# One four-tile buffer for all eight residual tiles, and a third weight load moved to ScalarE's queue

## What is computed

```python
grouped = x.reshape(b, s // g, g, d)                       # groups of g = 32 tokens
logits = jnp.einsum('bntd,des->bntes', grouped, Wc) + bc + tie
perm = (logits == jnp.max(logits, axis=-3, keepdims=True)) # each expert picks one token per group
permuted = jnp.einsum('bntd,bntes->bnesd', grouped, perm)  # gather
inner = jax.nn.relu(jnp.einsum('bnesd,esdf->bnesf', permuted, W1) + b1)
result_permuted = jnp.einsum('bnesf,esdf->bnesd', inner, W2) + b2
result = jnp.einsum('bnesd,bntes->bntd', result_permuted, perm)  # scatter
x = x + jnp.tanh(g_ffn[0]) * result                        # the residual sum
```

## Time and profile before

| | |
|---|---|
| median of 3 executions | 1777.69 us (1773.9 to 1778.45) |
| time of the profiled execution | 1778.45 us |
| its span in the profile | 1776.7 us |
| TensorE busy | 1663.9 us, 94% |
| VectorE busy | 1335.7 us, 75% |
| expert stage | from about 764 us of the span to its end |
| one iteration of it | about 62 us |

### The profile page before, as it was taken

One profiled execution on the slowest core, in us unless ns is written; L12 is line 12 of the kernel. 1 busy time (PEld: TensorE's weight loads), 2 busy tenths in 40 slices (PEclk: granted clock), 3 DMA queues, 4 the chain that ended last, 5 costly groups with the idle time before them and its releaser, 6 DMA issues.

```text
span 1776.7 us, 53886 instructions
## 1 busy us (share of the span) xinstructions
PE 1663.9 (94%) x23384; PEld 1184.5 (67%) x23384; DVE 1335.7 (75%) x1974; ACT 822.0 (46%) x1073; POOL 623.2 (35%) x847
## 2 busy tenths in 40 slices
PE   7899999999999999979999999999999999999985
PEld 4677777777777777776576567657656765765662
DVE  6777777777777777737788778778877877787776
ACT  3433333333333333445555555565555556555542
POOL 3577777777777777410110011011011101100101
PEclk9999999999999999989999999999999999999997
DMA  7345454545555545353675575576457556645754
GB/s 263 130 144 167 144 173 151 178 151 183 159 167 155 168 144 176 120 187 104 227 238 156 197 247 178 184 236 234 155 200 249 177 194 227 241 150 201 247 180 155
DMA packets 161450, 325.90 MB, mean 183 GB/s; under 512 B 17344, under 2 KB 23232, under 8 KB 155840
## 3 DMA queue, kind: packets, MB, share of 16 engines
q1 hardware_dynamic: 156608, 288.91, 49.9%
q10 hardware_dynamic: 4608, 33.56, 4.8%
HBM read 254.25 MB, written 68.16 MB: 181 GB/s over the span
## 4 chain that ended last, share of the span: by engine, by line
PE 57%; DVE 15%; POOL 10%; issue 9%; ACT 5%; DMA 2%; SPq 0%; DVEq 0%; POOLq 0%; ACTq 0%
PE ps L1309 13%; PE ps L1282 8%; PE ps L1336 8%; PE ps L214 6%; PE ps L844 6%; PE ps L1351 4%; POOL qc L486 4%; POOL qc L487 4%; PE ps L200 4%; PE ps L1331 3%; DVE mx L612 2%; DVE qs L629 2%; PE ps L807 2%; DVE qc L628 2%; PE ps L787 2%
## 5 line engine op out<-in xcount | busy, mean ns | idle before, releaser
L182 POOL TENSOR_TENSOR b_va<-b_mv,eps_layer 128x2 f32<-128x2 f32 x64 | 12.5, 196 | 833.6 <-DVE b_mv L173 832.7
L1194 DVE STREAM_TRANSPOSE res<-res 128x2048 f32<-128x2048 f32 x128 | 292.0, 2295 | 0.1
L1146 ACT ACTIVATE gat<-ps 128x1536 f32<-128x1536 f32 (+1 forms) x128 | 172.2, 1345 | 198.2 <-PE ps L1282 198.2
L787 PE MATMUL ps<-xTh,qh 128*128 128x512 f32 x512 | 208.6, 407 | 7.0 <-DVE qs L629 5.4
L787 PE MATMUL ps<-xTl,qh 128*128 128x512 f32 x512 | 200.2, 391 | 0.0
L787 PE MATMUL ps<-xTh,ql 128*128 128x512 f32 x512 | 199.8, 390 | 0.0
L1216 DVE COPY res<-ps 128x1024 f32<-128x1024 f32 x128 | 156.7, 1224 | 43.7 <-PE ps L1336 43.7
L1282 PE MATMUL ps<-sel,xin 32*128 32x128 f32 x4096 | 153.7, 283 | 27.9 <-ACT sel L242 13.5
L1156 ACT ACTIVATE res<-ps 128x1024 f32<-128x1024 f32 x128 | 131.2, 1025 | 92.8 <-PE ps L1336 92.8
L1282 PEld LDWEIGHTS ps<-sel,xin 32*128 32x128 f32 x4096 | 129.4, 186 | 63.0 <-ACT gat L1146 40.1
L475 POOL TENSOR_TENSOR xTl<-xT,xTh 128x512 fp32r<-128x512 f32 x128 | 160.7, 1286 | 10.9 <-ACT xTh L522 10.9
(11 more groups left out here) (132 smaller groups left out, 3217.1 us busy)
## 6 DMA issues: line engine op xcount, KB each, us to landing
xin<-x_scratch SPq DMA_DIRECT2D x196, 256.0 KB, 4.0
xT<-in_xT SPq DMA_DIRECT2D x32, 1024.0 KB, 5.9
xin<-in_x SPq DMA_DIRECT2D x64, 512.0 KB, 3.8
x_scratch<-xin SPq DMA_DIRECT2D x64, 512.0 KB, 3.1
xin<-in_W SPq DMA_DIRECT2D x128, 256.0 KB, 3.5
gat<-in_W ACTq DMA_DIRECT2D x32, 1024.0 KB, 8.5
xT<-in_W SPq DMA_DIRECT2D x68, 256.0 KB, 4.0
gat<-in_W SPq DMA_DIRECT2D x64, 256.0 KB, 3.8
```

Source lines behind the costliest of these rows:

```text
L787: last = e.matmul(ps[:, 2 + n % 2, :], a[:, c, n * DH:(n + 1) * DH], b[:, c, :], start=(k == 0), stop=(k == len(parts) - 1))
L1146: e.activation(o, v, ACT.Copy).then_inc(m_gaA.sem, 1)
L1194: e.transpose(v, v).then_inc(m_tr.sem, 1)
```

## The change

`NY`, the number of residual tiles with a place in `y`, was already four; now `y`'s four places serve all eight tiles of a batch. Tile t and tile t+4 use the same place, `y[:, t % NY]`. Tile t+4 can only be loaded once tile t has been stored from there. The count of uses, `use(b, t)`, takes the place of the batch number in the semaphores.

`spare(i + 1)` is thus free once the first product of batch i is done, and W2's part 7 is loaded whole by a third DMA on ScalarE's queue, after `t == 5` of the routing loop. `load_third` goes.

On SP the order in an iteration becomes: stores of tiles 0 to 3, loads of tiles 4 to 7, stores of tiles 4 to 7.

Batch 14 (`B - 2`) is an exception: its tiles 4 to 7 go to `xn[:, 0:4]`, and the tiles 4 to 7 of batch 15 go to `xn[:, 4:8]`. All eight are loaded by `load_late` in iteration 15, ahead of the stores, as soon as the last gathers have read `xn`.

```diff
-        NV, NY = route.NV, TH
+        NV, NY = route.NV, 4
...
+        use = lambda b, t: 2 * b + t // NY if b < B - 1 else 2 * B - 3
-        tile_of = lambda b, t: y[:, t] if t < NY else spare(b)[:, (t - NY) * D:(t - NY + 1) * D] if b < B - 1 else xn[:, t]
+        tile_of = lambda b, t: xn[:, t - NY] if b == B - 2 and t >= NY else y[:, t % NY]
...
         def load_second(e, i, u):
-            e.wait_ge(m_w1.sem, m_w1.at(i, 5))
+            e.wait_ge(m_w1.sem, m_w1.at(i, 7 if u == W2_MOVED[2] else 5))
             e.dma_start(second(i, u), w2_dram[u].rearrange("p (k d) -> p k d", d=D)).then_inc(d_room[u].sem, 16)
...
             def load_middle(i, c):
                 if i:
-                    e.wait_ge(d_ys[c].sem, d_ys[c].at(i - 2))
+                    e.wait_ge(d_ys[c].sem, d_ys[c].at(use(i - 2, NY + c)))
                     e.wait_ge(m_w2.sem, m_w2.at(i - 1, 5))
...
             def load_y(b, t):
+                k = use(b, t)
                 if t < NY and live(b + 1):
                     e.wait_ge(m_w1.sem, m_w1.at(b + 1, piece(b + 1, W1_MIDDLE)))
-                    if b:
-                        e.wait_ge(d_ys[t].sem, d_ys[t].at(b - 1))
-                elif t < NY:
-                    e.wait_ge(d_ys[t].sem, d_ys[t].at(b - 1))
-                elif live(b + 1):
-                    e.wait_ge(m_w1.sem, m_w1.at(b + 1, 7))
-                else:
-                    e.wait_ge(m_gap.sem, m_gap.at(b, 2 * C - 1))
-                e.dma_start(tile_of(b, t), batch(x1_dram, b, t, 1)[:, 0]).then_inc(d_yl[t].sem, 16)
+                if k:
+                    e.wait_ge(d_ys[t % NY].sem, d_ys[t % NY].at(k - 1))
+                e.dma_start(y[:, t % NY], batch(x1_dram, b, t, 1)[:, 0]).then_inc(d_yl[t % NY].sem, 16)
+            def load_late(b, t):
+                k = t + (b == B - 1) * NY
+                e.wait_ge(m_gap.sem, m_gap.at(B - 1, 2 * C - 2 + k // TH))
+                e.dma_start(xn[:, k], batch(x1_dram, b, NY + t, 1)[:, 0]).then_inc(route.d_x[k].sem, 16)
...
-            def load_third(i, c):
-                if i:
-                    e.wait_ge(d_ys[NY + c].sem, d_ys[NY + c].at(i - 1))
-                else:
-                    e.wait_ge(m_w1.sem, m_w1.at(0, 7))
-                e.dma_start(quarter(spare(i + 1), c), quarter(w2_dram[W2_MOVED[2]], c)).then_inc(d_room[W2_MOVED[2]].sem, 16)
...
+                if i == B - 1:
+                    for t in range(NY):
+                        load_late(i - 1, t)
+                    for t in range(NY):
+                        load_late(i, t)
                 if live(i - 1) and i < B:
+                    for t in range(NY):
+                        store_y(i - 1, t)
                     for t in range(NY, NT):
-                        load_y(i - 1, t)
-                    for t in range(NT):
+                        if i < B - 1:
+                            load_y(i - 1, t)
+                    for t in range(NY, NT):
                         store_y(i - 1, t)
-                if live(i):
-                    for c in range(QUARTERS):
-                        load_third(i, c)
-            for t in range(NY, NT):
-                load_y(B - 1, t)
...
         def scalar(e):
-                    if live(i) and t in (1, 3):
+                    if live(i) and t in (1, 3, 5):
                         load_second(e, i, W2_MOVED[t // 2])
...
         def tensor(e):
             def outer(i, u):
                 if u in W2_MOVED:
-                    e.wait_ge(d_room[u].sem, d_room[u].at(i, d_room[u].per - 1))
+                    e.wait_ge(d_room[u].sem, d_room[u].at(i))
```

More of the change, by code:

```diff
@@ L963, in experts @@
         mark = lambda name, per=1, unit=1: Mark(top, nc, "b_" + name, per, unit)
-        d_yl, d_ys = ([mark(f"{n}{k}", 1, 16) for k in range(NT)] for n in ("yl", "ys"))
+        d_yl, d_ys = ([mark(f"{n}{k}", 1, 16) for k in range(NY)] for n in ("yl", "ys"))
         d_mid = [mark(f"mid{c}", 1, 16) for c in range(QUARTERS)]
-        d_room = {u: mark(f"room{u}", 1 if u < W2_MOVED[2] else QUARTERS, 16) for u in W2_MOVED}
+        d_room = {u: mark(f"room{u}", 1, 16) for u in W2_MOVED}
         m_gap, m_w1, m_w2, m_sc = mark("gap", 2 * C), mark("w1", 2 * C), mark("w2", 8), mark("sc", NT)
@@ L969, in experts @@
         m_gaV, m_evV, m_tr, m_fin = mark("gaV", 2 * C), mark("evV", 8), mark("tr", 8), mark("fin", NT)
-        d_last = mark("last", 4, 16)
+        d_late, d_last = mark("late", NY, 16), mark("last", 4, 16)
         m_gate, m_add, m_end = mark("gate", 3), mark("add", 3), mark("end", 2)
@@ L1042, in landed_last @@
         def landed_last(e, h):
-            for t in range(NY * h, NY * h + NY):
-                e.wait_ge(d_yl[t].sem, d_yl[t].at(B - 1))
+            for t in range(NY):
+                d = route.d_x[NY + t] if h else d_yl[t]
+                e.wait_ge(d.sem, d.at(B if h else use(B - 1, t)))
         def sync(e):
@@ L1069, in load_y @@
             def load_y(b, t):
+                k = use(b, t)
                 if t < NY and live(b + 1):
                     e.wait_ge(m_w1.sem, m_w1.at(b + 1, piece(b + 1, W1_MIDDLE)))
-                    if b:
-                        e.wait_ge(d_ys[t].sem, d_ys[t].at(b - 1))
-                elif t < NY:
-                    e.wait_ge(d_ys[t].sem, d_ys[t].at(b - 1))
-                elif live(b + 1):
-                    e.wait_ge(m_w1.sem, m_w1.at(b + 1, 7))
-                else:
-                    e.wait_ge(m_gap.sem, m_gap.at(b, 2 * C - 1))
-                e.dma_start(tile_of(b, t), batch(x1_dram, b, t, 1)[:, 0]).then_inc(d_yl[t].sem, 16)
+                if k:
[5 more added lines that the diff above has]
+                e.dma_start(xn[:, k], batch(x1_dram, b, NY + t, 1)[:, 0]).then_inc(route.d_x[k].sem, 16)
             def store_y(b, t):
                 e.wait_ge(m_fin.sem, m_fin.at(b, t))
-                e.dma_start(batch(out, b, t, 1)[:, 0], tile_of(b, t)).then_inc(d_ys[t].sem, 16)
-            def load_third(i, c):
-                if i:
-                    e.wait_ge(d_ys[NY + c].sem, d_ys[NY + c].at(i - 1))
-                else:
-                    e.wait_ge(m_w1.sem, m_w1.at(0, 7))
-                e.dma_start(quarter(spare(i + 1), c), quarter(w2_dram[W2_MOVED[2]], c)).then_inc(d_room[W2_MOVED[2]].sem, 16)
+                d = d_late if b == B - 2 and t >= NY else d_ys[t % NY]
+                e.dma_start(batch(out, b, t, 1)[:, 0], tile_of(b, t)).then_inc(d.sem, 16)
             for i in range(B + 1):
@@ L1123, in sync @@
                 e.dma_start(batch(out, B - 1, 4 * h, 4)[:, :, rest_of], tiles_of_last(h)[:, :, rest_of]).then_inc(d_last.sem, 16)
-            for t in range(NT):
-                e.wait_ge(d_ys[t].sem, d_ys[t].at(B - 2))
+            for k in range(NY):
+                e.wait_ge(d_ys[k].sem, d_ys[k].at(use(B - 2, k)))
+            e.wait_ge(d_late.sem, d_late.at(0, NY - 1))
             e.wait_ge(d_last.sem, d_last.at(0, 3))
@@ L1203, in finish @@
                 e.wait_ge(m_sc.sem, m_sc.at(i, t))
-                e.wait_ge(d_yl[t].sem, d_yl[t].at(i))
+                if i == B - 2 and t >= NY:
+                    e.wait_ge(route.d_x[t - NY].sem, route.d_x[t - NY].at(B))
+                else:
+                    e.wait_ge(d_yl[t % NY].sem, d_yl[t % NY].at(use(i, t)))
                 v = tile_of(i, t)
```

## The result

| | before | changed |
|---|---|---|
| median of 4 executions | 1775.8 us | 1835.4 us |
| lowest to highest | 1773.1 to 1778.5 | 1829.6 to 1839.5 |
| span in the profile | 1776.7 | 1828.2 |

The ratio is 1.033, with a 95% interval of 1.029 to 1.038. The direction was forecast, the size was not: 1805 was predicted, and 1835 lies above the range of 1779 to 1826.

What follows compares the result with a forecast made beforehand. TensorE, busy 94% of the span, was taken to bound the kernel. Stalls of 31.6 us less a 4.5 us gain made +27.1 on 1778.45, so 1806, stated as a median of 1805; range 1779 to 1826.

Steps and rivals of the forecast that it cites:

- TensorE bounds the stage, with 2 us of cover ahead of `outer(·, 0)`: In the expert stage, TensorE delays the end; the residual sum has some 2 us to spare before `outer(·, 0)`.
- A W2 load in flight costs a residual transfer 3.1 us: On SP's queue, a 256 KB transfer beside a 1 MB W2 load takes 3.1 us, against 0.77 alone.
- Part 7's share, 31.6 - 12.4 = 19.2 us of stalls: Ahead of `outer(·, 0)`, W2's part 7 in flight behind part 6 raises the delay over 14 batches from 12.4 to 31.6 us.
- The new order and parts 5 and 6, 12.4 us: Lower bound of the delays ahead of `outer(·, 0)`: four batches at 3.1 us each, without part 7's added cost.
- The slots of before: Eight 256 KB transfers on SP's queue, landing times taken as unchanged: load 4+k lands where store k landed before.
- The sign named: In the changed trace, the four loads following the stores land 8 to 12 us after the first store's issue.
- the upper bound I took: Delays ahead of `outer(·, 0)` over 14 batches with part 7 behind part 6: 31.6 us, the value used.
- The 20 us put above it: Allowance for two residual slots paying 3.1 us instead of one, in ten batches, giving the top bound of 1825.
- The sorting of batches in three kinds: Batches 0 to 13 grouped by first W2 load's issue against SP's first store; upper delays 1.0, 2.1 and 4.3 us.
- The round trip of store and load: On SP, a load waiting for a store's landing pays a fresh DMA's round trip, 3.4 us at the shortest.
- the rival: TensorE stalls also lower the granted clock afterwards, costing up to 1.3 us more in eight batches: 1815 and up; chance 0.12.
- The last batch, -4.5, and up to 1.3 more: After batch 14's scatter, early residual loads shorten the 5.36 us stall, gaining 4.5 us; faster clock may return 1.3 more.

Runs made afterwards that it cites:

- the filler run: The changed kernel plus 16 transposes whose result nobody reads, on TensorE ahead of `outer(i, 0)` in iterations 1 to 14: 1822.7 us, ratio 1.026.
- the quarters: The changed kernel with each of ScalarE's three W2 loads cut into four column quarters, rows of 2 KB instead of 8 KB: 1777.5 us, ratio 1.0035.

## Why the prediction was right and wrong

- *TensorE bounds the stage, with 2 us of cover ahead of `outer(·, 0)`*: right. Where loads land early, as with the late W2 loads, nothing is lost.
- *Part 7 early removes no wait*: right. With it late again the kernel is faster.
- *A W2 load in flight costs a residual transfer 3.1 us*: right, 3.2 and 3.1 measured in batch 8. The cause was tested as well: it goes with the size of the rows on the other queue.
- *Part 7's share, 31.6 - 12.4 = 19.2 us of stalls*: 23.3 measured, from the run with part 7 late.
- *The new order and parts 5 and 6, 12.4 us*: 15.5 measured. The slots of before were too early a landing for the loads. The sign named was a landing 8 to 12 us after the first store's issue; in batch 8 the four loads landed 11.0 to 17.9 us after it, behind W2's parts 5, 6 and 7, where stores 0 to 3 of batch 7 had taken 5.5 to 13.7. The sum of the stalls was 38.8 instead of the 31.6 forecast; the upper bound I took was no upper bound. (The 20 us put above it were not worked out: 3.1 less 0.77 us in ten batches is 23.) The sorting of batches in three kinds did not last either: the changed kernel moves the phase of each iteration, and stalls came in 12 of the 14 batches.
- *The round trip of store and load*: I took it as a reason for the upper value. The run with all W2 loads late shows that it costs nothing on its own.
- **The step that failed: stalls of 3 to 4 us were costed without the granted clock.** The sum held nothing for it, and the rival had 0.12 and 10 us. It was 19.2 us, more than a third of the 51.5, or 1.7 us in each of 11 batches. That it is the clock is shown by the filler run and by the quarters, where it stayed up. I had set the rival low since no stall shorter than 5.36 us had shown a fallen clock. That was a wrong reading: the trace of before has shorter ones, at the start of the expert stage. After a wait of 2.15 us the clock fell, and 64 products of L1309 took 3.25 us instead of 2.09 at the full clock; after one of 4.04 us, which ended at 793.03, the clock of 791 to 798 reads 0.51. Counting the rival's own price of 1.3 us in 12 batches would have given 16, and 31.6 + 16 - 5.8 = 42 on 1778, or 1820. The start of the stage in the kernel before, and the clock there:

```profile
766.09 0.57 PE L1309 MATMUL ps<-gat,xT 128*64 128x64 f32 x13 [2.15 <-issue]
768.07 3.25 PE L1309 MATMUL ps<-gat,xin 128*64 128x64 f32 x64
```
```profile
767.00:771.00 4.00, 4.00 (x88) 3.78 (x85) 0.69 (x1) 1.45 (x1) 0.00 (x0) 0.57 0.72 232
```
- *The last batch, -4.5, and up to 1.3 more*: right. -5.4 in the profile, and 4.6 us for this part alone.
- *Together*: 38.8 + 19.2 - 5.4 - 1.1 = 51.5 in the profiled executions, against 31.6 + 0 - 4.5 = 27.1. Of the 24.4 us missed, 19.2 are the clock and 7.2 the stalls; the last batch and the rest take 2.0 off. The medians lie 60 apart rather than 51.5, as the profiled execution of the changed kernel (1830) was among the fastest of its runs and that of the kernel before (1778.45) the slowest of its four.

The Trainium skill speaks of both sides of the rows. In "DMA: Bandwidth & Descriptors", section "Queues, rings and completion order", an engine drains some number of descriptors from one queue and then turns to the next. A turn counted in descriptors gives the queue with the larger rows the larger share, and the three row sizes agree with that: bytes 3.3, 2.6 and 1.2 to 1. In "Perfetto Trace Analysis", section "DMA Optimizations", larger transfers are advised where bandwidth is the limit, and splitting where the DMA engines are mostly idle. Here they were full in that stretch, and still the same 1 MB in rows of 2 KB made the kernel 3% faster than in rows of 8 KB, since it was not the bulk load that anyone waited for; the measurement decides.

## What to carry to other kernels

When a transfer gets a new predecessor or neighbour, ask not only for its bytes but for who takes turns with it on the DMA engines: a bulk load with long rows that nobody waits for can slow short, urgent transfers on another queue fourfold (0.7 us between landings without it, 3.2 beside it). Move such a load behind the urgent ones, or cut it into columns so that its rows are as short as theirs. And when a forecast puts stalls of a few microseconds on TensorE, price the clock behind them as its own term; here it added half as much again to the stalls. Look for such stalls in the whole trace, also outside the stage that changes, before saying that none has shown a fallen clock.

## What was not expected of the hardware

- Work that is only filler can pay for itself: 16 transposes ahead of `outer(·, 0)` kept the granted clock at 1.00 instead of 0.72, and ten batches took 19 us less with them than without. In the first four batches the wait stood ahead of the filler, and it cost its own 14 us and gave nothing back.
- Waits of 2.15 to 3.3 us on TensorE were mostly followed by a clock of 0.5. Some were not: 2.6 us ahead of `outer` in batch 11 and 2.3 us ahead of L1311 at 1238.9 in the changed kernel, and 3.3 us in batch 10 of the kernel with filler. Why these differ stays open.
- Cutting a 1 MB load by partitions, 32 at a time, raised the time that its packets took from 7.3% to 10.7% of the engines' span for the same 50.3 MB, and the kernel went to 1916 us. Why these DMAs are slower stays open.
